# One bias product, one reordered group and W1 on x's queue, in the preparation of a graph attention layer

## The reference, cut to what matters

```python
h = jnp.maximum(_layernorm(x, axis=-1), 0.0)              # x is 4096 x 256
h = h @ W1 + b1                                           # W1 is 256 x 256
e = leaky_relu((h @ a1)[:, None] + (h @ a2)[None, :] + b2, 0.2)
attention = softmax(where(adj > 0, e, -1e12), axis=1)     # 4096 x 4096
x = x + elu(attention @ h)
```

## Time and profile before

| | |
|---|---|
| time, median of 3 runs | 424.49 us (424.48 to 424.57) |
| the profiled execution's own time | 424.74 us |
| its span | 423.0 us |
| TensorE busy | 415.9 us (98%) |
| VectorE busy | 374.5 us (89%) |
| ScalarE busy | 309.0 us (73%) |
| GpSimd busy | 24.9 us (6%) |
| first matmul of the main loop (line 745) | 49.3 us |

### The profile page before, as it was taken

How to read it: one execution, slowest core, us unless ns; L and a number is a source line. 1 busy time by engine, 2 the same in 40 slices (tenths; PEclk the granted TensorE clock), 3 DMA queues, 4 the chain that set the end, 5 groups by cost and what they waited for, 6 DMA issues and landing times.

```text
span 423.0 us, 8454 instructions
## 1 busy us (share of the span) xinstructions
PE 415.9 (98%) x3335; PEld 409.7 (97%) x3335; DVE 374.5 (89%) x404; ACT 309.0 (73%) x306; POOL 24.9 (6%) x44
## 2 busy tenths in 40 slices
PE   8899999999999999999999999999999999999996
PEld 7788899999999999999999999999999999999996
DVE  4887999999999399999995699999992999999955
ACT  4589898999983778867664889769574789586622
POOL 1011100000000400000000400000001200000003
PEclk9999999999999999999999999999999999999999
DMA  8950059555556436548388166747478165567302
GB/s 267 390 208 7 2 201 347 200 201 198 198 200 235 164 143 249 207 126 313 116 294 302 42 205 224 256 140 262 147 264 287 57 243 205 194 222 259 116 3 97
DMA packets 22585, 82.40 MB, mean 195 GB/s; under 512 B 1531, under 2 KB 14113, under 8 KB 14242
## 3 DMA queue, kind: packets, MB, share of 16 engines
q1 hardware_dynamic: 22276, 81.81, 54.8%
q10 hardware_dynamic: 286, 0.27, 0.2%
HBM read 77.86 MB, written 4.21 MB: 194 GB/s over the span
## 4 chain that ended last, share of the span: by engine, by line
PE 96%; DVE 2%; ACT 1%; issue 0%; POOL 0%; DVEq 0%; ACTq 0%; POOLq 0%
PE ps L772 53%; PE ps L774 26%; PE ps L653 5%; PE ps L794 2%; PE ps L795 2%; PE ps L796 2%; PE ps L641 2%; PE ps L595 1%; DVE adj_s L880 1%; DVE h_raw L865 0%; ACT hnT L434 0%; PE ps L621 0%; PE ps L612 0%; ACT xn L424 0%; DVE y L1087 0%
## 5 line engine op out<-in xcount | busy, mean ns | idle before, releaser
L774 PE MATMUL ps<-hp_lo,w_hi 128*128 (+1 forms) x936 | 226.8, 282 | 0.0
L772 PE MATMUL ps<-hp_hi,w_hi 128*128 (+1 forms) x936 | 226.7, 282 | 0.0
L880 DVE SCALAR_TENSOR_TENSOR adj_s<-R,p,adj_s 128x1024 f32<-128x1024 f32 x128 | 165.4, 1334 | 24.0 <-ACT adj_s L450 23.8
L772 PEld LDWEIGHTS ps<-hp_hi,w_hi 128*128 128x128 f32 x936 | 176.8, 189 | 0.0
L774 PEld LDWEIGHTS ps<-hp_lo,w_hi 128*128 128x128 f32 x936 | 176.6, 189 | 0.0
L458 ACT ACTIVATE w_hi<-adj_s 128x2048 fp32r<-128x2048 f32 x64 | 122.3, 1912 | 37.5 <-DVE adj_s L880 37.1
L890 DVE SCALAR_TENSOR_TENSOR w_lo<-adj_s,w_hi 128x2048 fp32r<-128x2048 f32 x64 | 146.2, 2285 | 0.0
L450 ACT ACTIVATE adj_s<-adj_s 128x2048 f32<-128x2048 int32 x64 | 122.3, 1911 | 25.6 <-DMA adj_s<-adj_t 25.3
L772 PE MATMUL ps<-hp_hi,w_lo 128*128 (+1 forms) x944 | 123.0, 283 | 0.0
L772 PEld LDWEIGHTS ps<-hp_hi,w_lo 128*128 128x128 f32 x944 | 117.3, 189 | 0.0
L653 PE MATMUL ps<-W1x,hnT 128*128 128x258 f32 x128 | 30.2, 381 | 0.4 <-ACT hnT L434 0.4
(11 more groups left out here) (110 smaller groups left out, 188.1 us busy)
## 6 DMA issues: line engine op xcount, KB each, us to landing
adj_s<-adj_t SPq DMA_DIRECT2D x64, 1024.0 KB, 4.9
x_s<-x SPq DMA_DIRECT2D x7, 512.0 KB, 8.5
o_s<-x SPq DMA_DIRECT2D x3, 1024.0 KB, 8.1
out<-o_s SPq DMA_DIRECT2D x6, 512.0 KB, 6.9
R<-r_rows SPq DMA_DIRECT2D x1, 1536.0 KB, 6.4
adj_s<-x SPq DMA_DIRECT2D x1, 1024.0 KB, 5.5
out<-adj_s SPq DMA_DIRECT2D x8, 128.0 KB, 1.7
x_s<-x SPq DMA_DIRECT2D x2, 256.0 KB, 3.9
```

The lines of the kernel that those rows point to most:

```text
L772: last = pe.matmul(acc, block_w, hh, start=fresh, stop=False)
L774: pe.matmul(acc, block_w, hl, start=False, stop=False)
L880: last = dve.scalar_tensor_tensor(sgn, R[:, ds(ic * CW, CW)], p[:, ds(source(r, c) + s, 1)], sgn, ALU.max, ALU.mult)
```

## The change

Five edits, all in the preparation.

W1's load moves from ScalarE's queue, where it was first, to SyncE's, third, behind x's second half-group. On ScalarE's queue the two small loads of the vectors are then first.

TensorE's two dummy matmuls that followed `turn_W1` now stand ahead of it.

The products of b1 with a1 and a2 go to GpSimd: three small instructions make `ab_sum`, 128 partial sums in two columns, with b2 added into the first row. `repeat_b1` goes. On TensorE `weigh_b1` (five matmuls) becomes `sum_ab` (one matmul that sums over the partitions), and moves from ahead of `transposes(1)` to behind it.

ScalarE's list is reordered: `keep_b1` moves behind `normalise(1)`, and `keep_ba` from ahead of `normalise(1)` to behind `relu_T(1)`.

VectorE's list is reordered: the second half of `statistics(2)` moves ahead of `invert(1)` and `normalise(1)`; its aggregation stays behind them, as `aggregate(2)`. Every aggregation now waits on a semaphore of its own.

```diff
@@ tiles @@
-        b1rep = over("b1rep", [P, KC, P], fp32, o_s, (KC + 1) * P * 4 + (3 * F + 8) * 4)
+        ab = sb("ab", [P, 2, KC])
+        ab_sum = sb("ab_sum", [P, 2])
@@ sync @@
             sp.dma_start(x_s[:, GT // 2:GT, :], x_v[:, GT // 2:GT, :]).then_inc(x_in[0], 16)
+            sp.dma_start(W1x[:, :, 0:F], W1.rearrange("(c p) f -> p c f", p=P)).then_inc(w_in, 16)
@@ gpsimd @@
+            pool.wait_ge(acol_kept, 3)
+            pool.tensor_tensor(ab[:, :, :], acol[:, A1:A2 + 1, :], acol[:, B1, :].unsqueeze(1).broadcast_to([P, 2, KC]),
+                               ALU.mult).then_inc(pool_c, 1)
+            pool.wait_ge(pool_c, 4)
+            pool.tensor_tensor(ab_sum[:, :], ab[:, :, 0], ab[:, :, 1], ALU.add).then_inc(pool_c, 1)
+            pool.wait_ge(pool_c, 5)
+            pool.wait_ge(row_in, 16)
+            pool.tensor_tensor(ab_sum[0:1, 0:1], ab_sum[0:1, 0:1], v_row[0:1, 3 * F:3 * F + 1], ALU.add).then_inc(ab_ready, 1)
@@ scalar @@
-            act.dma_start(W1x[:, :, 0:F], W1.rearrange("(c p) f -> p c f", p=P)).then_inc(w_in, 16)
...
             keep_acol()
-            repeat_b1()
             keep_WT()
             act.wait_ge(eps_ready, 1)
             root(0)
             normalise(0)
             keep_wv()
             relu_T(0)
+            root(1)
+            normalise(1)
             keep_b1()
-            root(1)
-            keep_ba()
-            normalise(1)
             root(2)
             relu_T(1)
+            keep_ba()
             normalise(2)
@@ tensor @@
-            def weigh_b1():
-
-                pe.wait_ge(acol_kept, 4)
+            def sum_ab():
+
+                pe.wait_ge(ab_ready, 1)
                 pe.wait_ge(hn_ready, KC)
-                for c in range(KC):
-                    pe.matmul(ps[:, SB, 0:2], b1rep[:, c, :], acol[:, A1:A2 + 1, c], start=c == 0, stop=False)
-                pe.matmul(ps[:, SB, 0:1], ones[0:1, 0:P], v_row[0:1, 3 * F:3 * F + 1], start=False, stop=True).then_inc(ba_ps, 1)
+                pe.matmul(ps[:, SB, 0:2], ones[:, :], ab_sum[:, :], start=True, stop=True).then_inc(ba_ps, 1)
...
             turn_vectors()
+            keep_warm(WARM[1])
             turn_W1()
-            keep_warm(WARM[1])
             weigh()
...
             project(0, 0)
-            weigh_b1()
             transposes(1)
+            sum_ab()
             pe.wait_ge(b1_kept, 1)
@@ vector @@
-                    link(last)
-                    for t in range(GT):
-                        dve.bn_aggr(agg[:, g, t, :], stats[:, g, t, :]).then_inc(agg_ready, 1)
+                    last.then_inc(stats_ready, 1)
+                    if aggregated:
+                        aggregate(g)
+
+            def aggregate(g):
+
+                dve.wait_ge(stats_ready, g + 1)
+                for t in range(GT):
+                    dve.bn_aggr(agg[:, g, t, :], stats[:, g, t, :]).then_inc(agg_ready, 1)
...
             statistics(2, 0)
+            statistics(2, 1, aggregated=False)
             invert(1)
             normalise(1)
-            statistics(2, 1)
+            aggregate(2)
             statistics(3, 0)
```

More of the change, by code:

```diff
@@ L175, in build @@
         acol_kept = sem("acol_kept")
+        ab_ready = sem("ab_ready")
         b1_ps = sem("b1_ps")
@@ L190, in build @@
         dve_c = sem("dve_c")
+        stats_ready = sem("stats_ready")
         agg_ready = sem("agg_ready")
@@ L383, in keep_acol @@
                 act.activation(acol[:, B1, :], cols[:, 2, :], ACT.Copy).then_inc(acol_kept, 1)
[L385 to L389, removed]
             def keep_WT():
@@ L827, in _, with statistics @@
             dve.memset(eps[:, :], EPS).then_inc(eps_ready, 1)
-            def statistics(g, hf):
+            def statistics(g, hf, aggregated=True):
                 if hf == 0:
```

## The result

The changed kernel is slower: 425.74 us, median of 22 executions, against 424.56 of 22 before; the ratio is 1.0036 with an interval of 1.002 to 1.0051. The forecast was 423.2.

A forecast was written before the change was run, and what follows sets the result against it. TensorE's solid matmul run from near 15.6 us was taken as the bound: +0.44 at the first group, transposes -1.47, sum_ab +0.22, so about -1.3 us. From the median 424.49 that gives 423.2 us, range 422.6 to 424.2.

The forecast's parts named there:

- What bounds the kernel: TensorE's full run from near 15.6 us; the stall behind keep_ba, about 2 us on ScalarE, can be taken out.
- not passed on: Rival: ScalarE or VectorE bounds 15 to 41 us, so the gain stops there; 424.2 to 424.6 us, chance 0.07.
- The swap, +0.44 us: Fillers ahead of W1's transposes: these end near 6.82 instead of 6.38, and all of group 0 moves 0.44 us back.
- the slower rival: TensorE idles from 6.8 to near 7.6 us, its clock falls back; 2.6 us lost, 425.8 us, chance 0.07.
- W1's landing, 5.4 us taken: W1, third on x's queue, lands at 5.4 us like the second half-group; bounds 4.6 and 7.2 us.
- The cover of 0.6 us: Slack between W1's assumed landing at 5.4 us and its transposes' first possible use near 6.0 us.
- the late W1: Rival: each 0.1 us W1 lands past 6.0 costs 0.1 us, up to 424.4 us; chance 0.13.
- Around the span: The execution's time outside its span: 1.74 us, kept unchanged in the forecast.
- The parts taken at nothing: Preparation work said to cost or gain nothing: repeat_b1's removal, GpSimd's products with over 6 us of cover, keep_ba, aggregate(2)'s wait.
- `sum_ab`: The one product behind group 1's transposes, on TensorE's path: 0.22 us, bounds zero and 0.68.
- The moved statistics: VectorE's second half of statistics(2) ahead of invert(1): costs about 0.35 us against taking invert(1) at once.
- the rival for more: invert(1) is not held and sum_ab hides: 0.35 + 0.22 us more gain, 422.6 us, chance 0.08.

The follow-up runs named there:

- e5: Changed kernel with W1's load back first on ScalarE's queue and the two filler matmuls back behind W1's transposes: 423.08 us, ratio 0.9966.
- e11: Kernel before with one edit, the two filler matmuls ahead of W1's transposes: 425.47 us, ratio 1.0036.
- e8: Changed kernel with W1's load third on ScalarE's queue, behind the vectors' two loads: 428.86 us, ratio 1.0077.
- e14: Changed kernel with SyncE waiting for W1's landing before it issues x's group 1: 424.35 us in one execution.
- e4: Changed kernel with W1's load first on ScalarE's queue and W1's transposes made to wait for x's group 1 too: 428.25 us, ratio 1.008.
- e2: Kernel before with one edit, W1's load third on x's queue: 431.26 us, ratio 1.0149.
- e17: Kernel before with the change's three small GpSimd instructions added, their result unused: 424.92 us, ratio 1.0007.
- e9: e5 with invert(1) and normalise(1) ahead of the second half of statistics(2): 423.0 us, ratio 0.9964.
- e18: Kernel before with ScalarE's new order and weigh_b1 moved ahead of weigh, no GpSimd products: 423.14 us, ratio 0.9968.
- e3: Changed kernel with 7 filler matmuls in place of 2 ahead of W1's transposes: 424.89 us, ratio 1.0005.
- e1: Changed kernel with W1's load put back first on ScalarE's queue, all else as changed: 423.71 us, ratio 0.9988.
- e6: Changed kernel with W1's load first on x's queue, ahead of both halves: 424.29 us, ratio 1.0009.

## Why the prediction was wrong

*What bounds the kernel*: right. The stall behind `keep_ba` was the one to take out, and the gain passed through to the main loop; the rival "not passed on" is out. e5, the reordering and the product without the two edits at W1, has a span 1.9 us shorter; the forecast for these parts was 1.3 + 0.44 = 1.74.

*The swap, +0.44 us*: the sign was right, the size is not settled. In e11's profiled execution `weigh` starts 0.22 us later than before (7.37 against 7.15), while the median of its eight executions that did not fall is 425.2, 0.7 us above before. What the term left out is the clock: the swap lengthens the wait ahead of `weigh` from 0.33 to 0.78 us, which I noted only under the slower rival.

*W1's landing, 5.4 us taken*: the step that failed first. It landed at 5.8 to 6.7, inside the bounds (4.6 to 7.2) but late of the figure. I took it from a load with the same bytes ahead of it and took those behind for harmless; e8 and the one execution of e14 speak against that. The cover of 0.6 us became a wait of up to 1.26 us.

*The slower rival, chance 0.07*: this is what most executions did, and what made the change slower; to set it aside was the step that decided. I had its mechanism and place, with 425.8 us for it (425.0 to 429.7 measured). I dismissed it by one row, the idle 1.24 us before 14.75 in the kernel before, after which the records ran at full rate. That row was true of its place, 7 us behind the clock's rise (near 6.2 by the prediction), and was carried to another, close behind it; e4 shows that as much idle time here does bring it down (six of six). That the distance from the rise makes the difference fits e2's second fall, but no run tests it. I also weighed the late W1 and the clock as separate cases with separate chances, when the first feeds the second. The Trainium skill (TensorE: Matmul & The Clock Gate, Part 1) names the sense of it: idleness brings the low rate back. The granted clock of 0.50 from 8.5 to 18 us agrees.

*Around the span*: taken as unchanged, 1.74 us. It is 2.19, by GpSimd's products (e17).

*The parts taken at nothing* (`repeat_b1`, GpSimd's products inside the span, `keep_ba`, the new wait of `aggregate(2)`) cost nothing inside the span that can be seen: e17 shows it for GpSimd's products, and for the others only the sum does, as e5's span gained no less than forecast. `sum_ab`, forecast at 0.22 us, took 0.23. The moved statistics, 0.35 us in the rival for more, cost nothing on TensorE's path, as e9 shows.

Still open: what exactly makes the clock fall in one execution and not in the next (1.26 us of wait for W1 held, 0.46 us fell, and e18 fell three times though its profiled execution has no long idle stretch), and by what path later loads delay an earlier one.

## What to carry to other kernels

Near the start, close behind the rise of TensorE's clock, count idle time at the price of the clock, not at its own length: in the profiled fall of the changed kernel 1.24 us of waiting (0.46 + 0.78) went with 3.9 us at the main loop's start, though as long or longer waits cost no more than themselves in other executions. Fillers belong into the wait itself (e3: none of 11 fell), and a load that gates them is better issued first than third (e5: none of 5). And look at more than one profile: three of them showed a kernel 0.8 to 1.0 us better in span, while its median time was 1.2 us worse.

## What the runs showed of the hardware

- W1, issued third, landed 3.6 us after its issue with no load behind it (one execution), and 4.1 to 5.0 with group 1 behind it on the same queue; as the last load of the other queue, with x's groups behind it on the first, it took 5.4. The Trainium skill (DMA: Bandwidth & Descriptors, Queues, rings and completion order) says that each DMA engine consumes a queue's descriptors in ring order. The trace agrees: in the first profile after the change the loads landed in the order of issue, x's halves at 3.6 and 4.4, W1 at 6.7 and group 1 at 8.1 us. The order alone does not tell how long each takes.
- Idle time of TensorE in the first 9 us can bring its clock from 2.4 back to 1.2 GHz for several us: all six executions fell with a made wait of 1.29 us besides the swap's (e4), none of 11 when dummy matmuls filled the wait (e3). With the swap's wait of 0.78 us and none for W1 in the profile, 3 of 12 (e1), 2 of 10 (e11) and 5 of 10 (e6) did.
- An execution with the three small GpSimd instructions is 0.38 us longer outside its span (2.18 against 1.80), whether or not their result is used.
- With only the schedule of the preparation changed, the spread of one kernel's executions went from 0.6 us to 5.7.
